# Token units of a fused four-layer network: second row products moved ahead of the scores, and encodings, statistics and loads moved behind the maxima

## The chip, the cores and the metric

The kernel runs on one core of a Trainium2 chip: TensorE (PE) multiplies matrices and writes PSUM, VectorE (DVE) and ScalarE (ACT) copy, subtract and normalize, GpSimd (POOL) does part of the splitting, SyncE (SP) issues the DMAs. The metric is device time in microseconds of the whole kernel, lower is better. Before the change the median of 3 runs is 2311.41 us (2311.12 to 2314.84).

## The reference

Two blocks of a network over 4 sequences of 512 positions; the code holds them as 8 halves of 256 tokens (`B, S = 8, 256`), each with its own causal attention. The change lies in the first part, four layers of attention over one-hot token codes plus position codes:

```python
enc = one_hot(token_ids) + sinusoidal_pe
def layer(enc, ws):
    wq, wk = ws
    q = enc @ wq
    k = enc @ wk
    sims = einsum('bqd,bkd->bqk', q, k) * scale
    sims = where(causal_mask, -1e9, sims)
    attn = softmax(sims, axis=-1)
    return einsum('bqk,bkd->bqd', attn, enc)
# four layers in a row, then
h = h + recurrent_attention(layernorm(h))
h = h + ternary_ffn(layernorm(h))
h = h + block_attention(layernorm(h))
h = h + table_ffn(layernorm(h))
```

## The kernel before

**Precision.** Every matrix product works on float16 pairs, a high half (ScalarE's copy) and a low half (VectorE's or GpSimd's subtraction of the high half from the float32 value), in three passes. So each product waits for a ScalarE copy and a subtraction behind it.

**Token units.** The 2048 tokens are 4 chunks c of 512. The four layers l of a chunk are units, 16 in all, in the order of the table `TOK`: (0,0) (0,1) (1,0) (0,2) (1,1) (2,0) (0,3) (1,2) (3,0) (2,1) (1,3) (2,2) (3,1) (2,3) (3,2) (3,3), as (l, c); unit 9 is (2,1). The layer's result is not formed; instead the attention matrices of a chunk are multiplied up (`tok_pt`), and each layer's q and k come from that product and "row products", encodings times the layer's weights (`tok_ew`, two halves b = 0 and 1, the second into PSUM bank 7). A token output (`tok_out`) multiplies the last product with the encodings of a chunk; `OUT_AT` places the four of them.

**One unit u, as each engine has it written out by hand.** The engines run their own lists in order and meet through semaphores.
- TensorE (`tok_pe`): project q and k of unit u+1 (`tok_project`, L461 and L464, or L250 for layer 0); first row products of u (L491, waits for the probabilities of u where it uses bank 2); transpose the probabilities of u (L272); scores of u+1 (`tok_scores`, L1523 and L1529, wait for `k_split`); second row products (L491); product of attention matrices (`tok_pt`, L507 to L511).
- ScalarE (`tok_act`): copies of q, k; outputs; encoding copies; a sum of |w| (`tok_act_abs`, L1621) in eight units, in units 1 and 6 (`ABS_LATE`) behind the exponential; first rows' copy (L1594); pT copy (L353); the split of a 1 MB weight piece in two halves (`rw_split_act`, L1501); second rows' copy (L1594); the exponential (`act_exp`, L305 and L307); the copy of `tok_pt`'s result (L1616).
- VectorE (`tok_dve`): low halves of q and k (L285, L289); column encodings (`cols_dve`, L1719); first rows' subtraction (L1708); pT's (L357); the mask and maxima of unit u+1 (`dve_max`, L295 to L299); second rows' subtraction; normalizing (`dve_norm`, L312 to L318, or `dve_norm_rows`, L399 to L412, for layer 0); the subtraction that ends `tok_pt` (L1743); column subtractions (`cols_lo`, L1727); row encodings (`rows_dve`, L1735; 2, 3, 3, 4, 4 in units 3 to 7); layer norm statistics (L574 to L582) and, in unit 12, mixing (L1461, L1471) for the next stage.
- GpSimd: low halves of the row encodings and of the weight piece (L1508). SyncE (queue SPq): per unit the next weight piece's two loads (L1883), its store (L1898), the 1 MB load for the sum of |w| (L1889), and the transposing DMAs of the probabilities (`sp_turn`, L386), four of 128x384 a turn.

Behind the units stands the recurrent attention stage, whose products (L749) bring TensorE to 99% busy. Its weights come by `load_rw`, a table lookup's indices by `load_idx`.

## Time and profile before

| | |
|---|---|
| median of 3 runs | 2311.41 us |
| profiled execution | 2310.06 us, span 2308.1 us |
| TensorE | busy 2232.7 us (97%) |
| VectorE | 1647.9 us (71%) |
| ScalarE | 718.5 us (31%) |
| GpSimd | 375.9 us (16%) |
| TensorE clock granted | 0.993 of full speed over the span |

The page divides the span in 40 slices of 57.7 us. TensorE has 6, 8, 7, 7 and 8 tenths in the first five and 9 or more in all others, so the time that can be won on it lies in the first 250 us: the token units. There DMA engines are busy 78% and ScalarE has two thirds of its stage filled.

### The profile page before, as it was taken

To read this page: it belongs to the slowest core of one execution; us is meant where nothing else is said; L and a number is where in the kernel's file an instruction comes from. 1 tells how busy PE (TensorE), PEld (TensorE's weight loads), DVE (VectorE), ACT (ScalarE), POOL (GpSimd) and SP (SyncE) were. 2 spreads that over 40 slices of the span, in tenths; PEclk is the share of its full clock that TensorE was granted. 3 is DMA by queue.
4 is the path that set the end of the run, shared out by engine and by line. 5 is a ranking of instruction groups with operands and counts; after the bars stand their busy time and mean duration, and the time that the engine had idled before them with its cause. 6 is when DMAs were issued, how large, how long until landed. Compare 5 with 4: busy or idle time off the path is not lost.

```text
span 2308.1 us, 31300 instructions
## 1 busy us (share of the span) xinstructions
PE 2232.7 (97%) x12058; PEld 1141.7 (49%) x12058; DVE 1647.9 (71%) x3357; ACT 718.5 (31%) x1603; POOL 375.9 (16%) x416
## 2 busy tenths in 40 slices
PE   6877899999999999999999999999999999999999
PEld 4666444444444444444445555555555555444444
DVE  7667799998998886577766665665665667688832
ACT  5666313122122122444333333233233233211111
POOL 3453100000000330541050002200300300401000
PEclk9999999999999999999999999999999999999999
DMA  6877533323332341120131112311311222100001
GB/s 171 264 194 206 216 132 119 128 96 119 133 120 93 142 154 67 44 85 12 51 94 35 35 30 52 89 31 32 107 33 31 71 46 35 60 1 1 1 1 74
DMA packets 171109, 196.47 MB, mean 85 GB/s; under 512 B 124368, under 2 KB 137296, under 8 KB 162000
## 3 DMA queue, kind: packets, MB, share of 16 engines
q1 hardware_dynamic: 170672, 193.41, 28.0%
q8 instruction: 96, 1.57, 0.3%
q10 hardware_dynamic: 288, 1.05, 0.1%
q14 instruction: 53, 0.43, 0.1%
HBM read 137.28 MB, written 27.26 MB: 71 GB/s over the span
## 4 chain that ended last, share of the span: by engine, by line
PE 85%; DVE 5%; issue 3%; ACT 2%; DMA 2%; POOL 1%; SPq 1%; DVEq 0%; POOLq 0%
PE ps L749 21%; PE ps L250 14%; PE ps L1370 10%; PE ps L761 7%; PE ps L1186 7%; PE ps L1173 7%; PE ps L642 5%; PE ps L1000 4%; PE ps L1017 3%; PE ps L1211 2%; PE ps L264 2%; PE ps L607 1%; PE ps L491 1%; SPq L386 1%; PE ps L1214 1%
## 5 line engine op out<-in xcount | busy, mean ns | idle before, releaser
L749 PE MATMUL ps<-planes 128*128 128x512 f16 x1224 | 270.0, 379 | 0.2 <-DVE work L806 0.2
L749 PE MATMUL ps<-planes,wa 128*128 128x512 f16 x1080 | 237.8, 379 | 0.4 <-DVE planes L1476 0.4
L250 PE MATMUL ps<-planes,wa 128*128 128x512 f16 x840 | 192.3, 379 | 3.2 <-DVE planes L1727 3.2
L749 PEld LDWEIGHTS ps<-planes 128*128 128x128 f16 x1224 | 119.6, 98 | 142.2 <-DVE work L806 1.1
L789 ACT ACTIVATE work<-work 128x512 f16<-128x512 f32 x64 | 40.3, 630 | 440.4 <-DVE work L822 440.4
L250 PE MATMUL ps<-planes 128*128 128x512 f16 x768 | 175.9, 379 | 0.9 <-DVE planes L622 0.9
L749 PEld LDWEIGHTS ps<-planes,wa 128*128 128x128 f16 x1080 | 105.6, 98 | 125.8 <-ACT h L1589 0.9
L305 ACT ACTIVATE ps<-ps,nmax 128x128 f32<-128x128 f32 x160 | 54.5, 341 | 307.0 <-DVE nmax L299 306.9
L587 POOL TENSOR_TENSOR rstd<-rstd,half 128x4 f32<-128x4 f32 x16 | 17.9, 1118 | 770.6 <-DVE rstd L582 770.5
L904 DVE COPY_PREDICATED work<-work 128x1024 f32<-128x1024 int16 x144 | 119.5, 830 | 20.9
L886 DVE TENSOR_SCALAR work<-work,lutx,par 128x256 int32<-128x256 int32 x384 | 128.0, 406 | 0.0
L250 PEld LDWEIGHTS ps<-planes,wa 128*128 128x128 f16 x840 | 80.6, 98 | 87.8 <-DVE planes L1727 3.8
L1017 PE MATMUL ps<-wa,work 128*128 128x512 f16 x512 | 120.9, 379 | 0.0
L1000 PE MATMUL ps<-planes,wa 128*128 128x512 f16 x512 | 120.6, 379 | 0.0
L1370 PE MATMUL ps<-planes 128*128 128x512 f16 x528 | 117.4, 379 | 0.0
L1370 PE MATMUL ps<-planes,wa 128*128 128x512 f16 x528 | 116.6, 379 | 0.0
L250 PEld LDWEIGHTS ps<-planes 128*128 128x128 f16 x768 | 73.8, 98 | 78.3 <-DVE planes L622 1.4
L1292 DVE TENSOR_TENSOR planes<-ps,planes 128x512 f16<-128x512 f32 x64 | 44.2, 691 | 81.0 <-ACT planes L1266 81.0
L970 POOL TENSOR_SCALAR planes<-stg 128x512 f16<-128x512 f32 x44 | 28.2, 669 | 446.3 <-PE ps L1186 368.6
L326 DVE RECIPROCAL rinv<-rsum 128x4 f32<-128x4 f32 x64 | 11.4, 178 | 117.5 <-ACT ps L307 115.4
L1298 DVE TENSOR_TENSOR h<-ps,h 128x512 f32<-128x512 f32 x64 | 44.2, 691 | 71.4 <-PE ps L1186 67.5
L761 PE MATMUL ps<-planes,work 128*128 128x512 f16 x408 | 93.6, 379 | 0.0
(195 smaller groups left out, 4242.4 us busy)
## 6 DMA issues: line engine op xcount, KB each, us to landing
planes<-rw SPq DMA_DIRECT2D x17, 2048.0 KB, 8.3
wa<-rw SPq DMA_DIRECT2D x15, 2048.0 KB, 7.3
stg<-in_rw_w SPq DMA_DIRECT2D x32, 512.0 KB, 5.6
stg<-in_ff_w SPq DMA_DIRECT2D x16, 1024.0 KB, 5.3
rw<-wa SPq DMA_DIRECT2D x16, 1024.0 KB, 8.0
stg<-in_mo_w SPq DMA_DIRECT2D x16, 1024.0 KB, 5.7
work<-in_glu_idx SPq DMA_DIRECT2D x48, 128.0 KB, 2.1
glu_dec<-work SPq DMA_DIRECT2D x48, 128.0 KB, 1.7
```

Source lines behind the costliest of these rows:

```text
L250: mm = te.matmul(ps[:, bank, :], w(i, kt), x(j, kt), start=(kt == 0 and n == 0), stop=(kt == KT - 1 and n == 2))
L305: se.activation(x, x, ACT.Exp, bias=nmax[:, b:b + 1], accum_out=rsum[:, b:b + 1])
L642: mm = te.matmul(ps[:, bank, :], x, y, start=(m == 0), stop=(m == len(pairs) - 1))
L749: mm = te.matmul(ps[:, what, :], rw_w(q, what, i, kt, m), mix[what][j][:, kt, at:at + CH], start=(kt == 0 and z == 0), stop=(kt == KT - 1 ...
L761: mm = te.matmul(ps[:, 4 + j, :], oT[t % 4][x][:, j * P:j * P + P], rw_wo(q, y, m), start=(n == 0 and z == 0), stop=(n == HEADS - 1 and z ...
L886: return ve.tensor_scalar(dec_v[:, j, :].bitcast(I32), dec_idx, lutx[:, j:j + 1], lut[:, 2 * j:2 * j + 1], ALU.bitwise_and, ALU.bitwise_xor)
L904: ins = ve.copy_predicated(pairs[:, :, 0, :], mask, pairs[:, :, 1, :])
L1000: mm = te.matmul(ps[:, t % 3, :], slot[:, at:at + P], tokT[x][:, kt, c * CH:c * CH + CH], start=(kt == 0 and x == 0), stop=(kt == KT - 1 a ...
L1017: mm = te.matmul(ps[:, 4 + j, :], gT[t % FF_BUF][x][:, j * P:j * P + P], slot[:, PW + m * D:PW + m * D + D], start=(k == 0 and x == 0), st ...
L1173: mm = te.matmul(ps[:, bank, :], tokT[x][:, kt, tt * P:tt * P + P], halves(slot, 2)[y][:, kt * CH:kt * CH + CH], start=(kt == 0 and z == 0 ...
L1186: mm = te.matmul(ps[:, FB, :], x, y, start=(z == 0), stop=(z == len(pairs) - 1))
L1370: mm = te.matmul(ps[:, 2 * (n % 2) + piece, :], glu_halves(g, piece)[i][:, at:at + P], tokT[j][:, kt, c * CH:c * CH + CH], start=(kt == 0 ...
```

## The change

1. TensorE: the second row products stand ahead of the scores of unit u+1. VectorE: the second rows' subtraction stands ahead of the maxima.
2. VectorE: column subtractions, row encodings and the layer norm statistics (moved from unit 9 to unit 10) stand between the maxima and the normalizing; the mixing of unit 12 stands behind the normalizing and `tok_pt`'s subtraction, and its two ScalarE copies behind `tok_pt`'s copy.
3. The probabilities' planes have another layout (768 contiguous columns for both sequences of a chunk), so a turn is two transposes of 128x768 instead of four of 128x384.
4. Unit 14's transposes write banks 6 and 7 and no longer wait for the previous `tok_pt`.
5. SyncE: in iterations 1 and 6 the load for the sum of |w| goes behind the weight loads and the store; weight pair 1 of the next stage is loaded after the last token output and the first index load.

```diff
@@ pe_transpose_probs, act_pT, dve_pT @@
+        def pT_bank(u):
+            return 6 if u == LAYERS * NC - 2 else 4
...
-                    mm = te.transpose(ps[:, 4 + b, i * P:i * P + P], prob[:, at:at + P], ident[:, :])
+                    mm = te.transpose(ps[:, pT_bank(u) + b, i * P:i * P + P], prob[:, at:at + P], ident[:, :])
@@ layout and transposes @@
+        def p_turn(half_, c, which):
+
+            at = c * NTOK + CH + which * 768
+            return planes[:, 4 + half_, at:at + 768]
...
             for half_ in range(2):
-                for b in range(2):
-                    dst = act_T(4 + half_)[:, 2 * b + 1 - src, c * CH:c * CH + 384].rearrange("p (n q) -> p n q", n=3)
-                    sp.dma_start_transpose(dst, act_T(4 + half_)[:, 2 * b + src, c * CH:c * CH + 384]).then_inc(done, 16)
+                sp.dma_start_transpose(p_turn(half_, c, 1 - src).rearrange("p (n q) -> p n q", n=6), p_turn(half_, c, src)).then_inc(done, 16)
@@ tok_pe @@
-                tok_scores(pe, u + 1, 2 * nth(l, c, (0, 1, 2)) - 1 if l < LAYERS - 1 and ew_bank(u, 0) == 2 else 0)
                 if l < LAYERS - 1:
                     tok_ew(pe, u, 1)
+                tok_scores(pe, u + 1, 2 * nth(l, c, (0, 1, 2)) - 1 if l < LAYERS - 1 and ew_bank(u, 0) == 2 else 0)
...
             u = MU - 2
+            pe.wait_ge(ew_lo, 2 * nth(*TOK[u - 1], (0, 1, 2)))
+            pe.wait_ge(to_free, 2 * TPC)
+            pe_transpose_probs(pe, u)
             pe.wait_ge(pt_lo, nth(*TOK[u - 1], (1, 2, 3)))
-            pe_transpose_probs(pe, u)
@@ tok_act @@
-                if u == MU - 4:
-                    mix_hi_act(act, 0)
-                    mix_hi_act(act, 1)
                 if u in ABS_LATE:
                     tok_act_abs(act, ABS_AT.index(u))
                 if l > 0:
                     tok_act_pt(act, u)
+                if u == MU - 4:
+                    mix_hi_act(act, 0)
+                    mix_hi_act(act, 1)
@@ tok_dve @@
                 tok_dve_pT(dve, u)
-                dve_max(dve, u + 1)
-                if u == 1:
-                    cols_lo(dve, COLS_AT[1])
                 if l < LAYERS - 1:
                     tok_dve_ew(dve, u, 1)
-                if u == MU - 4:
-                    mix_diff(dve, 0, 0)
-                    mix_y_dve(dve, 0)
-                    mix_y_dve(dve, 1)
+                dve_max(dve, u + 1)
+                if u > 0:
+                    cols_lo(dve, COLS_AT.get(u, ()))
+                for r in ROWS_AT.get(u, ()):
+                    rows_dve(dve, r)
+                if u == OUT_AT[0] + 1:
+                    dve.wait_ge(to_free, TPC)
+                    ln_dve_chunk(dve, 0, 0, chain)
                 tok_dve_norm(dve, u + 1)
                 if l > 0:
                     tok_dve_pt(dve, u)
-                if u > 1:
-                    cols_lo(dve, COLS_AT.get(u, ()))
-                for r in ROWS_AT.get(u, ()):
-                    rows_dve(dve, r)
-                if u == OUT_AT[0]:
-                    dve.wait_ge(to_free, TPC)
-                    ln_dve_chunk(dve, 0, 0, chain)
...
                 if u == MU - 4:
+                    mix_diff(dve, 0, 0)
+                    mix_y_dve(dve, 0)
+                    mix_y_dve(dve, 1)
                     mix_lo_dve(dve, 0)
@@ sync: load_rw and the loop of weight pieces @@
-                        sp.wait_ge(to_ps, 3 * TPC)
+                        sp.wait_ge(to_ps, NT)
...
-                if j in ABS_AT[:-1]:
+                if j in ABS_AT[:-1] and j not in ABS_LATE:
                     sp.wait_ge(abs_done, ABS_AT.index(j) + 1)
                     load_abs(ABS_AT.index(j) + 1)
...
                 store_rw(j)
+                if j in ABS_LATE:
+                    sp.wait_ge(abs_done, ABS_AT.index(j) + 1)
+                    load_abs(ABS_AT.index(j) + 1)
...
-            load_rw(1)
             store_rw(RW_PIECES - 1)
...
-            load_rw(2)
             sp.wait_ge(mix_lo, 12)
             sp.wait_ge(to_free, NT)
             load_idx(0)
+            load_rw(1)
+            load_rw(2)
             load_rw(3)
```

In the changed kernel the lines are shifted: L1708 is L1719, L1727 is L1738, L1735 is L1746, L295 to L299 are L301 to L305, L491 is L500, L1523 is L1532, L1529 is L1538.

VectorE in unit 1, before: low halves of q and k, two column encodings, the first rows' subtraction, then the maxima and two column subtractions, and only then the second rows' subtraction.

```order
L285 SCALAR_TENSOR_TENSOR work<-ps,work 128x512
L289 TENSOR_TENSOR work<-ps,work 128x512
L1719 SCALAR_TENSOR_TENSOR work<-h,work 128x512 x2
L1708 TENSOR_TENSOR h<-ps,h 128x2x256
L295 TENSOR_TENSOR ps<-ps,causal 128x256
L295 TENSOR_TENSOR ps<-ps,causal 128x2x128
L298 TENSOR_REDUCE nmax<-ps 128x2
L299 TENSOR_REDUCE nmax<-ps 128x2
L1727 TENSOR_TENSOR planes<-work,planes 128x512 x2
L1708 TENSOR_TENSOR h<-ps,h 128x2x256
```

After:

```order
L291 SCALAR_TENSOR_TENSOR work<-ps,work 128x512
L295 TENSOR_TENSOR work<-ps,work 128x512
L1730 SCALAR_TENSOR_TENSOR work<-h,work 128x512 x2
L1719 TENSOR_TENSOR h<-ps,h 128x2x256 x2
L301 TENSOR_TENSOR ps<-ps,causal 128x256
L301 TENSOR_TENSOR ps<-ps,causal 128x2x128
L304 TENSOR_REDUCE nmax<-ps 128x2
L305 TENSOR_REDUCE nmax<-ps 128x2
L1738 TENSOR_TENSOR planes<-work,planes 128x512 x2
```

Both subtractions of the row products now stand in one row, ahead of the maxima.

VectorE in unit 7 around the normalizing of unit 8, before: maxima, second rows' subtraction, reciprocal and normalizing, the subtraction of `tok_pt`, and the last four row encodings (L1735) ahead of the low halves of q and k of unit 9.

```order
L295 TENSOR_TENSOR ps<-ps,causal 128x256
L295 TENSOR_TENSOR ps<-ps,causal 128x2x128
L298 TENSOR_REDUCE nmax<-ps 128x2
L299 TENSOR_REDUCE nmax<-ps 128x2
L1708 TENSOR_TENSOR h<-ps,h 128x2x256
L312 RECIPROCAL rinv<-rsum 128x4
L316 TENSOR_TENSOR work<-ps,rinv 128x2x128
L318 TENSOR_TENSOR work<-ps,rinv 128x2x256
L1743 TENSOR_TENSOR planes<-ps,planes 128x2x384
L1735 SCALAR_TENSOR_TENSOR work<-work 128x512 x4
L285 SCALAR_TENSOR_TENSOR work<-ps,work 128x512
L289 TENSOR_TENSOR work<-ps,work 128x512
```

After, the four encodings (L1746) stand between the maxima and the reciprocal:

```order
L1719 TENSOR_TENSOR h<-ps,h 128x2x256
L301 TENSOR_TENSOR ps<-ps,causal 128x256
L301 TENSOR_TENSOR ps<-ps,causal 128x2x128
L304 TENSOR_REDUCE nmax<-ps 128x2
L305 TENSOR_REDUCE nmax<-ps 128x2
L1746 SCALAR_TENSOR_TENSOR work<-work 128x512 x4
L318 RECIPROCAL rinv<-rsum 128x4
L322 TENSOR_TENSOR work<-ps,rinv 128x2x128
L324 TENSOR_TENSOR work<-ps,rinv 128x2x256
L1754 TENSOR_TENSOR planes<-ps,planes 128x768
L291 SCALAR_TENSOR_TENSOR work<-ps,work 128x512
L295 TENSOR_TENSOR work<-ps,work 128x512
```

What moved is four encodings, from between normalizing and q and k to between maxima and normalizing.

TensorE in unit 5 (row products of the unit around the transposes and scores), before:

```order
L250 MATMUL ps<-planes,wa 128x512 x24
L491 MATMUL ps<-wa,planes 128x256 x24
L272 MATMUL ps<-ident,work 128x128 x6
L1523 MATMUL ps<-work 128x256 x6
L1529 MATMUL ps<-work 128x128 x6
L491 MATMUL ps<-wa,planes 128x256 x24
L507 MATMUL ps<-work,planes 128x256 x3
```

After:

```order
L250 MATMUL ps<-planes,wa 128x512 x24
L500 MATMUL ps<-wa,planes 128x256 x24
L278 MATMUL ps<-ident,work 128x128 x6
L500 MATMUL ps<-wa,planes 128x256 x24
L1532 MATMUL ps<-work 128x256 x6
L1538 MATMUL ps<-work 128x128 x6
L516 MATMUL ps<-work,planes 128x256 x3
```

The 24 matmuls of the second row products now stand between the transposes and the scores.

## Rows read from the trace of the kernel before

**Rows 1.** Busy time by stretch: start:end us, its length, then each engine's busy us

```profile
0.00:250.80 250.80, 187.44 (x1530) 141.24 (x1531) 177.43 (x313) 162.11 (x325) 105.98 (x93) 0.93 0.78 218
250.80:2308.10 2057.30, 2045.25 (x10528) 1000.45 (x10528) 1470.44 (x3044) 556.39 (x1279) 269.88 (x324) 1.00 0.23 69
```

**Rows 2.** Who TensorE waited for, first 300 us: us in total, times, longest us

```profile
PE ps L1523 <- DVE work L289: 13.8, 10, 4.0
...
PE ps L539 <- DVE planes L1743: 7.0, 3, 4.9
```

**Rows 3.** Timeline of unit 9: start us, us, engine, line, tiles, count [idle before <- releaser]

```profile
156.49 2.78 PE L491 MATMUL ps<-wa,planes 128*128 128x256 f16 x24
...
159.11 0.82 PE L272 MATMUL ps<-ident,work 128*128 128x128 f32 x6
...
167.58 2.78 PE L491 MATMUL ps<-wa,planes 128*128 128x256 f16 x24 [0.46 <-DVE work L318]
...
160.67 1.99 ACT L1501 ACTIVATE wa<-stg 128x1024 f16<-128x1024 f32 x2
...
163.85 0.60 ACT L1594 ACTIVATE h<-ps 128x512 f16<-128x512 f32 x1 [1.19 <-PE ps L491]
...
165.84 0.22 ACT L307 ACTIVATION_READ_ACCUMULATOR ps<-ps,nmax 128x1 f32 x1
...
161.68 0.76 DVE L295 TENSOR_TENSOR ps<-ps,causal 128x256 f32<-128x256 f32 x2
...
162.81 0.68 DVE L299 TENSOR_REDUCE nmax<-ps 128x2 f32<-128x512 f32 x1
```

**Rows 4.** Transposes (ns min/median/max), a wait for a load, the page's landing time

```profile
L386 SPq DMA_TRANSPOSE planes<-planes x48: 1197/1260/2856, 30.5 to 229.4; - x48
...
L347 SPq DMA_TRANSPOSE work<-work x64: 1274/1432/2318, 1182.3 to 1949.0; - x64
...
89.84 1.91 ACT L1621 ACTIVATE stg<-stg 128x2048 f32<-128x2048 f32 x1 [2.91 <-DMA stg<-in_ff_w]
...
planes<-rw SPq DMA_DIRECT2D x17, 2048.0 KB, 8.3
```

**Rows 5.** Timeline of VectorE: encodings twice, statistics, mixing

```profile
124.25 2.73 DVE L1735 SCALAR_TENSOR_TENSOR work<-work 128x512 f32<-128x512 f32 x4
...
139.67 3.63 DVE L1735 SCALAR_TENSOR_TENSOR work<-work 128x512 f32<-128x512 f32 x4
...
168.11 2.46 DVE L574 BATCH_NORM_STATS2 stat<-h 128x6 f32<-128x512 f32 x4
...
201.62 3.08 DVE L1471 SCALAR_TENSOR_TENSOR work<-work,par 128x512 f32<-128x512 f32 x2
```

**Rows 6.** Timeline of TensorE: landmarks of the token stage

```profile
72.12 2.78 PE L491 MATMUL ps<-wa,planes 128*128 128x256 f16 x24 [2.90 <-DVE planes L412]
...
87.61 1.37 PE L1523 MATMUL ps<-work 128*128 128x256 f16 x6 [2.13 <-DVE work L289]
...
100.59 2.78 PE L491 MATMUL ps<-wa,planes 128*128 128x256 f16 x24
...
144.64 1.44 PE L1523 MATMUL ps<-work 128*128 128x256 f16 x6 [3.96 <-DVE work L289]
...
180.06 2.78 PE L491 MATMUL ps<-wa,planes 128*128 128x256 f16 x24 [0.46 <-DVE work L318]
...
207.20 5.71 PE L539 MATMUL ps<-planes 128*128 128x512 f16 x18 [4.94 <-DVE planes L1743]
...
250.81 15.70 PE L749 MATMUL ps<-planes,wa 128*128 128x512 f16 x72 [0.43 <-DVE planes L1476]
```

**Rows 7.** Timeline of unit 1: ScalarE, VectorE, and TensorE's next project

```profile
50.11 1.06 ACT L1501 ACTIVATE wa<-stg 128x1024 f16<-128x1024 f32 x1 [2.04 <-DMA stg<-in_rw_w]
...
46.73 0.76 DVE L295 TENSOR_TENSOR ps<-ps,causal 128x256 f32<-128x256 f32 x2
...
51.47 5.35 PE L250 MATMUL ps<-planes,wa 128*128 128x512 f16 x24 [2.41 <-DVE planes L1727]
```

More of the change, by code:

```diff
@@ L265, in pe_scores, with pT_view @@
             mm.then_inc(scored, 1)
+        def pT_bank(u):
+            return 6 if u == LAYERS * NC - 2 else 4
+        def pT_view(u):
+            return ps[:, pT_bank(u):pT_bank(u) + 2, 0:384]
         def pe_transpose_probs(pe, u):
@@ L347, in sp_pT @@
             sp.dma_start_transpose(pT_all, prob_all).then_inc(pT_in, 16)
-        pT_view = ps[:, 4:6, 0:384]
+        pt_view = ps[:, 4:6, 0:384]
         def act_pT(act, u):
             act.wait_ge(pT_ps, nth(*TOK[u], (1, 2, 3)))
-            se.activation(pT[0].rearrange("p (b k) -> p b k", b=2), pT_view, ACT.Copy).then_inc(pT_hi, 1)
+            se.activation(pT[0].rearrange("p (b k) -> p b k", b=2), pT_view(u), ACT.Copy).then_inc(pT_hi, 1)
         def dve_pT(dve, u):
             dve.wait_ge(pT_hi, nth(*TOK[u], (1, 2, 3)))
-            ve.tensor_tensor(pT[1].rearrange("p (b k) -> p b k", b=2), pT_view,
+            ve.tensor_tensor(pT[1].rearrange("p (b k) -> p b k", b=2), pT_view(u),
                              pT[0].rearrange("p (b k) -> p b k", b=2), ALU.subtract).then_inc(pT_split, 1)
@@ L376, in build @@
         TOK_W = wa[:, 8192:16384].rearrange("p (i l q k d) -> p i l q k d", i=2, l=LAYERS, q=2, k=KT)
+        def p_turn(half_, c, which):
+            at = c * NTOK + CH + which * 768
+            return planes[:, 4 + half_, at:at + 768]
         def chunk_rows(half_, c, which):
-            return act_T(4 + half_)[:, which:which + 3:2, c * CH:c * CH + 384]
+            return p_turn(half_, c, which).rearrange("p (b k) -> p b k", b=2)
         def sp_turn(sp, c, src, done):
             for half_ in range(2):
-                for b in range(2):
-                    dst = act_T(4 + half_)[:, 2 * b + 1 - src, c * CH:c * CH + 384].rearrange("p (n q) -> p n q", n=3)
-                    sp.dma_start_transpose(dst, act_T(4 + half_)[:, 2 * b + src, c * CH:c * CH + 384]).then_inc(done, 16)
+                sp.dma_start_transpose(p_turn(half_, c, 1 - src).rearrange("p (n q) -> p n q", n=6), p_turn(half_, c, src)).then_inc(done, 16)
         def sp_p1(sp, u):
@@ L422, in p_rows @@
         def p_rows(half_, c, b):
-            return act_T(4 + half_)[:, 2 * b, c * CH:c * CH + 384]
+            return p_turn(half_, c, 0)[:, b * 384:b * 384 + 384]
         def p_cols(half_, c, b):
-            return act_T(4 + half_)[:, 2 * b + 1, c * CH:c * CH + 384]
+            return p_turn(half_, c, 1)[:, b * 384:b * 384 + 384]
         def ew_tile(l, half_, tt):
@@ L453, in tok_project @@
             if l == 1:
-                pe.wait_ge(p1T_in[c], 64)
+                pe.wait_ge(p1T_in[c], 32)
             else:
@@ L502, in tok_pt @@
             else:
-                pe.wait_ge(pr_in[c], 64 * (l - 1))
+                pe.wait_ge(pr_in[c], 32 * (l - 1))
             for b in range(2):
@@ L1615, in tok_act_pt @@
             act.wait_ge(pt_ps, nth(*TOK[u], (1, 2, 3)))
-            se.activation(chunk_rows(0, TOK[u][1], 1), pT_view, ACT.Copy).then_inc(pt_hi, 1)
+            se.activation(chunk_rows(0, TOK[u][1], 1), pt_view, ACT.Copy).then_inc(pt_hi, 1)
         def tok_act_abs(act, k):
@@ L2041, in _ @@
                 rw_split_pool(pool, u)
-                if u == OUT_AT[0]:
+                if u == OUT_AT[0] + 1:
                     ln_pool_chunk(pool, 0, 0)
```

2 lines of the change are left out of this document (1 added, 1 removed).

## The prediction, made before the changed kernel ran

> **What bounds the kernel now.** I read four views. First the busy time by stretch: the change lies in the first 250.8 us, the token stage, where TensorE is busy 187.44 of 250.80 us at a mean granted clock of 0.93; in the 2057.30 us behind it TensorE is busy 99% and nothing is moved there that it waits for [rows 1]. So the question is how much of the 63 us of idle time and of the low clock goes. Second, who waits for whom: TensorE's largest repeated wait is at the scores, which need VectorE's low half of k: 13.8 us in 10 waits [rows 2], and into it the change puts row products, 2.78 us a unit (2.63 from start to the next start) [rows 3]. Third, the timeline of one unit that has no such wait (unit 9, [rows 3]): what closes its loop. Fourth, TensorE's landmarks over the stage [rows 6], which my sum runs along.
>
> In unit 9 before, from the start of the first row products (156.49) to the same point of unit 10 (167.58) it takes 11.1 us. ScalarE takes the rows' copy, pT and the two halves of the weight split (160.67, 1.99 us), and then stands until TensorE has ended the second row products (163.85); only behind that copy does the exponential begin. VectorE's maxima (161.68 to 162.81 + 0.60 = 163.4) were done beside it, hidden. The exponential ends at 166.06, and behind VectorE's normalizing TensorE goes on at 167.58 [rows 3].
>
> **The change part by part.** *Row products before the scores, their subtraction before the maxima.* No instruction more or less. In the new order unit 9 goes: first rows' end 2.63 us after their start (159.12), ScalarE's copy, pT and split end as now at 162.66; the second rows are then done (156.49 + 2.63 + 0.66 + 2.63 = 162.4, the transposes at 0.82 less what overlaps), so the copy runs 162.66 to 163.26; VectorE's subtraction 0.69 (as its maxima's second instruction of the same size, 0.68), 163.95; scores are ready (162.4 + 1.2 = 163.6); maxima 1.74 (161.68 to 163.42 before), 165.7; exponential 1.7 (from the copy's end at 164.4 to 166.06), 167.4; normalizing and the signal to TensorE 1.5 (166.06 to 167.58), 168.9 [rows 3]. Overlaps of neighbouring instructions take some 0.1 off: the loop is 12.4 us instead of 11.1. So every unit with row products pays 1.3 us, since the maxima, once hidden, now stand on the loop behind ScalarE's split; it earns back its own wait at the scores, up to 2.63 us.
>
> *Work behind the maxima.* Encodings, column subtractions and the statistics now lie under the exponential, which covers 1.74 us. Four encodings take 3.63 us beside GpSimd, 0.91 each, while four others took 2.73, 0.68 each [rows 5]; I take 0.68 to 0.9. Statistics take 2.46 and some 0.5 for two short steps, 3.0 us [rows 5]. What exceeds 1.74 spills: 0.9 in unit 3 (two subtractions, two encodings, 2.6), 0.3 in units 4 and 5, 1.0 in unit 6, 1.5 in unit 7, 1.2 in unit 10. But they no longer stand ahead of the next q and k.
> On the 3.63 the Trainium skill (SBUF — State Buffer, "Who interferes with whom") says that a VectorE instruction with two SBUF inputs contends with a GpSimd instruction that reads SBUF. By it all moved encodings that meet GpSimd's split would run at the long time, some 1 us more a unit in units 5 to 7, which is the slow rival below.
>
> *Transposes.* 24 issues instead of 48. Issue time: 1260 ns for 384 columns, 1432 ns for 1536 [rows 4]; at 768 I take 1.3, with 2.5 (in proportion) as the upper end and 1.26 as the lower. SP then gives 2.6 us instead of 5.2 a turn. The first turn holds TensorE now and would land some 2 us earlier, but the next thing that holds TensorE (unit 1, below) does not hang on it, so on the path it is worth 0 us. With 2.5 each SP is as late as now: 0 to +1.5 us.
> The Trainium skill (DMA: Bandwidth & Descriptors) tells in its table on transposes between SBUF tensors that earlier generations push one command per tile, 32 cycles a tile. Twelve tiles against three cost 172 ns more here, so the trace agrees in kind; by it a six-tile issue would be some 1.34 us, and the sum stays.
>
> *Loads.* The weight loads go before the load for the sums of |w| in iterations 1 and 6. ScalarE waits for that load twice, in units 2 and 4, the second time 2.91 us [rows 4]: the first stays (its load follows a sum that now comes later), the second goes, as SP is free in time. The load of the second weight pair waits for the last token tile and goes behind the first index load; the product that reads it starts behind 72 others, at 250.81 + 15.70 = 266.5 [rows 6], and issued at about 253 with a landing of 8.3 us [rows 4] it has 5 us to spare: 0 us. The index load goes earlier by about 3 us; TensorE is busy there without a gap, so 0 us.
>
> **The sum along TensorE's landmarks** [rows 6]; each is the time before plus the running difference.
> *Unit 1: +3.9.* Here the reorder costs most. VectorE had maxima at 46.73 and the column subtractions right behind, which TensorE's project at 51.47 waits for. Now the second rows' subtraction stands ahead of both, and its copy on ScalarE waits behind a weight half that lands at 50.1: 51.65 [rows 7]. Then 0.69 + 1.74 + 1.3 (two column subtractions of the same size, GpSimd done by then): 55.4 with the signal instead of 51.47. TensorE then stands some 9 us and will run at the lower clock for a while; that lies in the wait of unit 2, so I count 0, upper end +2.
> *Unit 2: +1.3*, no wait to earn. *Unit 3: +0.8*: 1.3 + 0.9 spill − 1.4 of waits. Running +6.0.
> *Unit 4: −4.4.* TensorE's own chain bound it: a wait of 2.13 before the scores, low clock behind it (six take 1.37, as against 0.8 elsewhere; 1.8 with the row products behind them), 1.0 for the pT delayed by the load [rows 4, 6]; against a new wait of 0.5 at the end. Running +1.6.
> *Units 5 and 6: +1.6 and +0.3.* Running +3.5.
> *Units 7 and 8: −3.5.* The four encodings of 3.63 us stood before q and k of unit 9, so that its scores waited until 144.64 [rows 5, 6]; this goes, less the spill and 1.3. Running 0.
> *Unit 9: +1.0. Unit 10: +1.2* (statistics spill; its scores' wait of 1.5 is paid out in the loop). Running +2.2 at 180.06. *Unit 11: −1.1*: there the exponential waits for the layer norm transposes anyway, so the maxima are hidden.
> *Unit 12: −2.9.* The mixing (to 201.62 + 3.08 = 204.7 [rows 5]) stood before the normalizing; now behind. The token output starts at 205.4, not 207.20. Running −1.8.
> *Unit 13: +3.1.* The mixing is now ahead of the copies, ScalarE's outputs wait for it as before (each output sits behind a mixing copy), a 1.9 us sum of |w| follows, and then the new order costs its 1.3. It gives nearly all back; running +1.3 at the normalizing of unit 14. *Unit 14: −1.0*: its transposes no longer wait for the previous subtraction. Running +0.3, and this reaches 250.81.
>
> 3.9 + 1.3 + 0.8 − 4.4 + 1.6 + 0.3 − 3.5 + 1.0 + 1.2 − 1.1 − 2.9 + 3.1 − 1.0 = +0.3. The profiled execution took 2310.06 us, 1.96 beside its span; with +0.3 it is 2310.4. The median of the runs is 1.35 above the profiled one, so the forecast is 2311.7 us: no change. About 0.2%, 4.6 us, is what a measurement of this kernel can tell from none.
>
> **The rivals.** *All waits are filled and the maxima stay hidden.* If ScalarE's part of the loop shortens too (its split often waited for weights, and loads now come earlier), the units do not pay 1.3. The nine units from 2 on that have second rows, but for unit 11, times 1.3 is 11.7 us off, and unit 1 may be 2 less: 2298; half of it 2304. For it: 13.8 us of waits, 7.0 more at the token output [rows 2]. Against: in unit 9 the split did not wait and the loop still closes through it. Chance 0.29.
> *Spill: the work behind the maxima delays the normalizing (slower).* In units 3 to 7 and 10 the moved work runs beside GpSimd's split, each instruction at 0.91 or more instead of 0.68; with 17 such instructions and 4 subtractions, 21 × 0.25 = 5, and 2 of low clock in unit 1: 2319. It decides as soon as VectorE reaches the reciprocal more than 1.74 us after its maxima. For it: 3.63 for four, 2.46 for the statistics [rows 5]. Against: GpSimd's split ends before the late part. Chance 0.22.
> *The change does not do what it says* in units 0 (already so), 8, 12, 14 and 15, which have no second row products: true, and in the sum.
> The forecast's case has 0.49.
>
> **How the numbers follow.** The forecast's case spans 2306 to 2317 (each unit ±0.4 over thirteen, and the two ends of transposes and clock). The range reaches into both rivals: 2301 to 2320. Faster by over 0.2% needs under 2306.8: the first rival and an edge of the forecast, 0.31. Slower needs over 2316: 0.22. Within: 0.47.
>
> **What would show it.** Right: the scores' waits of 13.8 us fall below 4; waits on the normalizing's output (before the first rows or the transposes) rise to over 12; the project of unit 2's iteration starts near 55, token output 1 near 205; transposes issue in about 1.3. In a plain unit the exponential starts about 2.5 us after ScalarE's second row copy has ended. Wrong: if that project starts before 52, unit 1 is mis-sized; if the loop of unit 9 stays at 11.1 us, the first rival holds; if the normalizing in units 5 to 7 starts over 1 us after the exponential's end, the second.

## The result, and the profile after

The kernel after takes 2320.6 us (median of 8 runs, 2317.6 to 2322.4), the kernel before 2311.4 (8 runs, 2310.0 to 2314.8): a ratio of 1.0038, 95% interval 1.0028 to 1.0047. It is slower by 9.2 us. The forecast was 2311.7 with a range of 2301 to 2320, so the result lies just outside it. The two profiled executions, from which all rows come, took 2321.28 and 2310.06 us and so lie 11.2 apart.

First the busy time by stretch of the kernel after, columns as in [rows 1]:

```profile
0.00:262.08 262.08, 191.78 (x1531) 143.76 (x1531) 176.76 (x313) 160.56 (x326) 104.01 (x93) 0.90 0.69 201
262.08:2319.30 2057.22, 2045.26 (x10528) 1000.57 (x10528) 1471.86 (x3044) 555.99 (x1277) 269.28 (x324) 1.00 0.23 70
```

All of it lies in the token stage, which ends at 262.08 in place of 250.81 [rows 1]. The 2057 us behind it have not moved. Of the 11.3 us TensorE is busy 4.3 longer with the same matmuls, at a mean granted clock of 0.90 in place of 0.93, and stands idle 6.9 longer.

Who TensorE waited for after (us in total, times, longest us), first 300 us:

```profile
PE ps L278 <- DVE work L324: 11.8, 4, 5.5
...
PE ps L500 <- DVE planes L421: 9.2, 2, 5.0
PE ps L250 <- DVE planes L1738: 8.0, 2, 7.2
PE ps L278 <- DVE planes L1754: 7.3, 2, 6.2
PE ps L500 <- DVE work L324: 5.5, 3, 3.2
...
PE ps L1532 <- DVE work L295: 2.1, 3, 1.5
```

The same waits before:

```profile
PE ps L491 <- DVE planes L412: 4.8, 2, 2.9
...
PE ps L250 <- DVE planes L1727: 3.2, 2, 2.4
...
PE ps L272 <- DVE work L318: 1.9, 1, 1.9
...
PE ps L491 <- DVE work L318: 0.9, 2, 0.5
```

The wait at the scores went from 13.8 us to 2.1 [rows 2], as foretold. In its place stand longer ones: 26.5 us in place of 7.6 for the normalizing (L324 and L421; into the transposes L278 and the first row products L500), and 8.0 in place of 3.2 for the column subtractions (L1738) at the project (L250), of which 7.2 in unit 1.

TensorE's landmarks after. 79.36, 106.86, 151.42, 190.74, 215.19 and 262.08 are the points that [rows 6] have at 72.12, 100.59, 144.64, 180.06, 207.20 and 250.81; 56.22 is the project of [rows 7], and 164.79 the start of unit 9's row products in [rows 3]:

```profile
56.22 7.58 PE L250 MATMUL ps<-planes,wa 128*128 128x512 f16 x24 [7.21 <-DVE planes L1738]
...
79.36 7.97 PE L500 MATMUL ps<-wa,planes 128*128 128x256 f16 x48 [5.01 <-DVE planes L421]
...
95.61 0.85 PE L278 MATMUL ps<-ident,work 128*128 128x128 f32 x6 [2.69 <-DVE work L324]
...
106.86 2.78 PE L500 MATMUL ps<-wa,planes 128*128 128x256 f16 x24 [0.29 <-DVE work L324]
...
121.37 7.07 PE L500 MATMUL ps<-wa,planes 128*128 128x256 f16 x48 [4.16 <-DVE planes L421]
...
150.08 1.54 PE L278 MATMUL ps<-ident,work 128*128 128x128 f32 x6 [6.16 <-DVE planes L1754]
...
151.42 1.49 PE L1532 MATMUL ps<-work 128*128 128x256 f16 x6
...
159.22 5.73 PE L548 MATMUL ps<-planes 128*128 128x512 f16 x18 [2.23 <-DVE planes L1754]
164.79 2.78 PE L500 MATMUL ps<-wa,planes 128*128 128x256 f16 x24
...
177.21 2.78 PE L500 MATMUL ps<-wa,planes 128*128 128x256 f16 x24 [2.07 <-DVE work L324]
...
190.74 4.29 PE L500 MATMUL ps<-wa,planes 128*128 128x256 f16 x24 [3.18 <-DVE work L324]
...
215.19 3.40 PE L548 MATMUL ps<-planes 128*128 128x512 f16 x15 [2.23 <-DVE planes L1754]
...
262.08 15.70 PE L758 MATMUL ps<-planes,wa 128*128 128x512 f16 x72 [0.74 <-ACT h L1600]
```

Two more rows of the kernel before, the transposes of unit 4 and the token output of unit 9:

```profile
84.67 0.82 PE L272 MATMUL ps<-ident,work 128*128 128x128 f32 x6
...
152.60 4.04 PE L539 MATMUL ps<-planes 128*128 128x512 f16 x18 [1.34 <-DVE planes L1743]
```

Read the second column (how long the group took) beside the wait in the brackets. The project takes 7.58 us behind a wait of 7.21, where [rows 7] have 5.35 behind 2.41. 48 row products take 7.97 and 7.07 us behind waits of 5.01 and 4.16; where the clock is up, 48 take 5.40 (e4 below). Six transposes take 1.54, not 0.87, and the token output 5.73, not 4.04. In those two stretches of row products, and around the project, the granted clock by window was 0.67, 0.76 and 0.71: a part of each group ran at 1.2 GHz and the rest at 2.4.

And unit 1, whose entry in the sum, +3.9, was the largest on the side of loss: ScalarE's second row copy, VectorE's subtraction behind it, and the column subtractions that the project waits for:

```profile
51.93 0.58 ACT L1605 ACTIVATE h<-ps 128x512 f16<-128x512 f32 x1
...
52.54 0.69 DVE L1719 TENSOR_TENSOR h<-ps,h 128x512 f16<-128x512 f32 x1 [5.79 <-ACT h L1605]
...
54.88 1.28 DVE L1738 TENSOR_TENSOR planes<-work,planes 128x512 f16<-128x512 f32 x2
```

### The profile page after: what moved, and what is told of

Same layout as the page of the kernel before. It is cut to its first block, busy times and chain, and to the rows that moved or that the text cites. A ratio compares the mean times of both kernels' runs of the same rounds, so it can differ in the third digit from the quotient of the medians.

```text
span 2319.3 us, 31281 instructions
## 1 busy us (share of the span) xinstructions
PE 2237.0 (96%) x12058; PEld 1144.3 (49%) x12058; DVE 1648.6 (71%) x3357; ACT 716.5 (31%) x1603; POOL 373.3 (16%) x416
## 4 chain that ended last, share of the span: by engine, by line
PE 86%; DVE 5%; ACT 4%; issue 3%; DMA 1%; POOL 1%; SPq 0%; DVEq 0%; POOLq 0%; ACTq 0%
PE ps L758 21%; PE ps L250 14%; PE ps L1379 10%; PE ps L770 7%; PE ps L1195 7%; PE ps L1182 7%; PE ps L651 5%; PE ps L1009 4%; PE ps L1026 3%; PE ps L1220 2%; PE ps L264 2%; PE ps L500 1%; PE ps L616 1%; PE ps L1223 1%; PE ps L262 1%
## 5 line engine op out<-in xcount | busy, mean ns | idle before, releaser
L250 PE MATMUL ps<-planes,wa 128*128 128x512 f16 x840 | 194.5, 382 | 8.0 <-DVE planes L1738 8.0
L250 PE MATMUL ps<-planes 128*128 128x512 f16 x768 | 175.9, 379 | 0.9 <-DVE planes L631 0.9
L250 PEld LDWEIGHTS ps<-planes,wa 128*128 128x128 f16 x840 | 81.2, 99 | 94.1 <-DVE planes L1738 8.5
L250 PEld LDWEIGHTS ps<-planes 128*128 128x128 f16 x768 | 73.8, 98 | 78.3 <-DVE planes L631 1.4
```

The lines of the kernel that those rows point to most:

```text
L250: mm = te.matmul(ps[:, bank, :], w(i, kt), x(j, kt), start=(kt == 0 and n == 0), stop=(kt == KT - 1 and n == 2))
```

## The experiments

Sixteen kernels, each against runs of the kernel before on the same chip. "Before" was 2310.6 to 2311.7 us in all of them. A "filler" is a matmul whose result nobody reads. The table below has, for the kernels before and after and five of the sixteen, the time in us from the start of ScalarE's exponential of unit u to that of unit u+1, read from the timeline of ScalarE. The last step goes from exponential 15 to the first product behind the stage.

| step of unit | before | after | e6 | e4 | e1 | e3 | e15 |
|---|---|---|---|---|---|---|---|
| 1 | 14.93 | 18.19 | 15.49 | 17.59 | 15.27 | 15.62 | 15.47 |
| 2 | 15.89 | 19.70 | 19.03 | 18.67 | 19.81 | 19.20 | 15.43 |
| 3 | 13.32 | 16.48 | 13.83 | 13.98 | 13.41 | 13.32 | 13.32 |
| 4 | 15.02 | 11.75 | 13.35 | 12.68 | 11.46 | 12.82 | 11.99 |
| 5 | 12.67 | 13.11 | 13.39 | 13.39 | 13.68 | 13.67 | 13.78 |
| 6 | 12.91 | 15.52 | 15.52 | 13.85 | 16.18 | 12.90 | 12.90 |
| 7 | 14.55 | 12.71 | 10.84 | 12.70 | 10.58 | 11.27 | 12.93 |
| 8 | 12.70 | 10.97 | 13.73 | 10.30 | 13.77 | 12.70 | 12.71 |
| 9 | 15.74 | 18.74 | 16.82 | 17.05 | 17.41 | 15.74 | 15.73 |
| 10 | 12.47 | 12.42 | 12.17 | 12.41 | 11.09 | 12.48 | 12.48 |
| 11 | 15.30 | 16.42 | 19.26 | 16.55 | 17.27 | 15.29 | 15.29 |
| 13 | 20.11 | 20.12 | 18.51 | 20.12 | 18.99 | 21.09 | 19.00 |
| 14 | 13.31 | 12.83 | 12.65 | 12.89 | 12.63 | 13.44 | 12.64 |
| end | 16.90 | 17.94 | 17.92 | 17.94 | 16.97 | 16.69 | 17.02 |

(Unit 0 takes 12.98 and unit 12 8.37 in all.) Each column is one execution, and a step can differ by chance. In e7, below, every engine has the instructions of the kernel before up to unit 12, and yet its unit 5 took 14.32 us where before has 12.67. So a difference of 1.7 in one step proves little; the medians of the runs carry the verdicts.

**e1: the order back, the moves kept.** The kernel after with

```diff
-                if l < LAYERS - 1: tok_ew(pe, u, 1)
                 tok_scores(pe, u + 1, ...)
+                if l < LAYERS - 1: tok_ew(pe, u, 1)
...
-                if l < LAYERS - 1: tok_dve_ew(dve, u, 1)
                 dve_max(dve, u + 1)
+                if u == 1: cols_lo(dve, COLS_AT[1])
+                if l < LAYERS - 1: tok_dve_ew(dve, u, 1)
```

> The kernel after, with the old order of the two parts that the change swapped: TensorE takes the next unit's scores before the second row products, and VectorE the maxima before the second rows' subtraction (in unit 1 the encodings' subtractions stand right behind the maxima, as before). The moved encodings, statistics, mixing, loads and the two-transpose form stay. Theory A (the order and the TensorE clock that its longer waits cost are the loss; the moved work fits behind the maxima): the loss of 9.2 us goes and a little more, 2304 to 2312 us. Rival B (the moved encodings behind the maxima hold up the normalizing and are the loss): it stays slow, 2316 to 2321 us. Rival C (transposes or loads): the same 2316 to 2321.

Measured: 2313.4 us, ratio 1.0009 (1.0000 to 1.0018). That lies outside both expectations, 1.4 us over the first. Seven of the 9 us are the order. The spill as the whole cause falls; but the kernel isn't below before, so something among the moves costs as well.

**e2: the order back in unit 1 alone.** The same edit under `if u == 1`.

> The kernel after, with the old order in unit 1 alone, on TensorE and VectorE. The ledger had unit 1 at +3.9 us, without the lower clock of the project behind it (7.58 us in place of 5.35). Theory A: 4 to 6 us less than after, 2314.5 to 2316.5 us, with the project of unit 3 back near 51.5 and at 5.4 us. Rival B (spill in later units absorbs it): under 2 us less than after, 2319 to 2321 us.

Measured: 2317.3 us, 1.0023 (1.0012 to 1.0034), 3.3 less than after, between the two. In its trace the project started at 50.50 and took 5.35, 5.7 us earlier; but unit 2 then took 21.09 in place of 19.70, and the row products of unit 3 took 8.27. (That profiled execution, 2321.2 us, was the slowest of seven, 3.9 over their median.) What ate most of the gain in unit 2 is a load, by this trace: ScalarE stood for the feed-forward piece that the change had moved behind the row weights' loads:

```profile
63.25 1.91 ACT L1635 ACTIVATE stg<-stg 128x2048 f32<-128x2048 f32 x1 [6.77 <-DMA stg<-in_ff_w]
```

In the kernel after the same piece is waited for 1.17 us, since TensorE is late there itself; e9 and e10 take the load up.

**e4: the waits filled with matmuls.**

```diff
+            for z in range(FILL[u]):      # {3: 40, 6: 34, 8: 48}
+                te.matmul(ps[:, 6, 0:S]..., tokT[0][:, 0, 0:P], TOK_W[:, 0, 3, :, 0, :], start=True, stop=True)
...
+                if u == 1:
+                    for z in range(30):
+                        te.matmul(ps[:, 0, :], TOK_W[:, 0, 0, 0, 0, :], tokT[0][:, 0, 0:CH], start=True, stop=True)
```

> The kernel after, with matmuls whose result nobody reads put on TensorE into four of its waits: 30 of 512 columns ahead of the project of unit 3 (a wait of 7.2 us), 40, 34 of 256 columns ahead of the first row products of units 3 and 6 (5.0 and 4.2 us) and 48 ahead of the transposes of unit 8 (6.2 us). At the full clock they take about 6.4, 4.3, 3.7 and 5.2 us, less than the waits. Theory A (the clock that the longer waits cost is the part of the loss that the ledger counted as nothing): the project, row products and transposes behind them run at the full clock, 7.58 -> 5.35, 7.97 -> 5.4, 7.07 -> 5.4, and of these 5 to 6 us most reach the end: 2314 to 2317 us. Rival D (the work behind the waits is slow for another reason, or its length is hidden by VectorE and ScalarE): within 1.5 us of after, 2319 to 2322 us. Cost of a filler that runs past its wait: up to 2 us slower.

Measured: 2314.0 us, 1.0010 (1.0002 to 1.0019). Its timeline of TensorE, fillers (L1550) and landmarks:

```profile
55.61 5.35 PE L250 MATMUL ps<-planes,wa 128*128 128x512 f16 x24
...
72.56 4.53 PE L1550 MATMUL ps<-wa,planes 128*128 128x256 f16 x40
77.72 5.40 PE L500 MATMUL ps<-wa,planes 128*128 128x256 f16 x48 [0.64 <-DVE planes L421]
...
114.11 3.87 PE L1550 MATMUL ps<-wa,planes 128*128 128x256 f16 x34
118.43 5.40 PE L500 MATMUL ps<-wa,planes 128*128 128x256 f16 x48 [0.44 <-DVE planes L421]
...
139.15 5.40 PE L1550 MATMUL ps<-wa,planes 128*128 128x256 f16 x48
...
153.94 4.04 PE L548 MATMUL ps<-planes 128*128 128x512 f16 x18 [2.22 <-DVE planes L1769]
...
183.77 4.42 PE L500 MATMUL ps<-wa,planes 128*128 128x256 f16 x24 [3.18 <-DVE work L324]
...
255.28 15.70 PE L758 MATMUL ps<-planes,wa 128*128 128x512 f16 x72 [0.71 <-ACT h L1615]
```

These extra 152 matmuls do nothing but keep TensorE at work, and the stage ends 6.8 us earlier. TensorE is busy 203.91 us in it; less the fillers' 20.4 by their rows, its own work takes some 183.5 us (an estimate) where after has 191.78. The steps tell where the end gains: units 1 and 2 (-1.6), 3 (-2.5), 4 (+0.9), 6 (-1.7), 8 and 9 (-2.4). Where nothing was filled (unit 11) the group behind a wait of 3.18 us is still slow, 4.42. So TensorE's clock behind the waits is a cause; filling four of them is worth 6.6 us.

Not all of a slow group's time reaches the end. The project at 55.61 takes 2.2 us less than after's at 56.22, but unit 2's step is only 1.0 shorter, because ScalarE now stands longer for the feed-forward piece (2.37 us, after 1.17):

```profile
63.97 1.91 ACT L1647 ACTIVATE stg<-stg 128x2048 f32<-128x2048 f32 x1 [2.37 <-DMA stg<-in_ff_w]
```

Nor can a slow group be put down to one wait. The token output of unit 9 takes 4.04 here and 5.73 in after, behind the same wait of 2.2 us. It is tempting to credit the fill of unit 8's wait, but other runs speak against it. In e12 that wait is filled too, the transposes behind it are fast, and the token output is slow (first fence); in e9 nothing is filled and it is fast behind 2.22 us (second); and in e16 24 row products are slow behind the 2.07 us behind which after has 2.78 (third):

```profile
145.36 0.87 PE L278 MATMUL ps<-ident,work 128*128 128x128 f32 x6 [1.13 <-DVE planes L1772]
...
153.83 5.73 PE L548 MATMUL ps<-planes 128*128 128x512 f16 x18 [2.23 <-DVE planes L1772]
```

```profile
151.19 4.05 PE L548 MATMUL ps<-planes 128*128 128x512 f16 x18 [2.22 <-DVE planes L1752]
```

```profile
173.50 4.45 PE L500 MATMUL ps<-wa,planes 128*128 128x256 f16 x24 [2.07 <-DVE work L324]
```

So the sum of the fills is shown, by medians; the share of unit 9 in it isn't.

**e5: the order alone, on the kernel before.** e1's edit in the other direction.

> The kernel before, with the swap of order alone, on TensorE (second row products, then scores) and on VectorE (second rows' subtraction, then the maxima); encodings, statistics, mixing, loads and transposes stay where they were. Theory A (the order is the loss): 2319 to 2326 us, at or above the kernel after, since nothing is moved behind the maxima to pay for it. Rival B (the moved encodings are the loss, not the order): 2309 to 2313 us.

Measured: 2326.3 us, 1.0064 (1.0051 to 1.0077): 14.6 us over before. That is 0.3 us past the upper end of the first expectation. The order alone costs more than the whole change; the rest of the change pays about 6 us back.

**e3: transposes and loads alone.** The kernel after with TensorE's, ScalarE's and VectorE's order of before.

> The kernel before in its own order on TensorE, VectorE and ScalarE, with the two wide transposes in place of four and the moved loads alone. The old-order kernel with every move of the change stood at 2313.4 us, 1.7 over the kernel before; either these parts cost it or the work moved behind the maxima. Theory A (the moved work behind the maxima costs those 1.7 us, the transposes and loads nothing, as forecast): 2310.5 to 2312.5 us. Rival C (transposes or loads cost it): 2313 to 2315 us.

Measured: 2308.4 us, 0.9989 (0.9980 to 0.9997): a gain of 2.6 us, outside both expectations. So these parts help, and in the old order the moved work costs the difference to e1, 5 us by the medians: units 6 (16.18 to 12.90), 9 and 11. In units 4, 10, 13 and 14 the moved work is ahead by 0.8 to 2.1 each; the two profiled executions are only 2.3 us apart.

**e6: VectorE's old order alone.**

> The kernel after, with VectorE alone in the old order (the maxima before the second rows' subtraction, in unit 1 the encodings right behind the maxima); TensorE keeps the new one. The sum made the loop 1.3 us longer per unit because the maxima stand behind ScalarE's copy and VectorE's subtraction of the second rows. Theory A, if that is so: the scores end 1.3 us after the second row products, the copy and the subtraction some 2.5 us after them, so the loop of a unit of four row-product blocks gets about 1 us shorter (12.4 -> 11.4) and the stage 4 to 7 us shorter: 2314 to 2317 us. Rival E (the later scores on TensorE set it, VectorE's order does not): 2318 to 2321 us.

Measured: 2316.2 us, 1.0020 (1.0011 to 1.0029), 4.4 less than after; the size came as expected, its place did not. The plain loop (unit 10) went from 12.42 to 12.17 only, so what lengthens it is TensorE's order: e1 differs from e6 in that alone, has 11.09 there, and is 2.8 us shorter in all. (The 12.47 of before in that step have the layer norm statistics in them, which stand ahead of the next q and k there.) The gain is in unit 1 (18.19 to 15.49) and behind it in unit 3, whose row products found the clock up after a shorter wait:

```profile
50.48 5.35 PE L250 MATMUL ps<-planes,wa 128*128 128x512 f16 x24 [3.23 <-DVE planes L1738]
...
76.02 5.40 PE L500 MATMUL ps<-wa,planes 128*128 128x256 f16 x48 [1.94 <-DVE planes L421]
```

**e7 and e8: fillers in the old order.** They stand ahead of two table products of the kernel before, and ahead of six groups of e1. (A table product is what the prediction calls a token output, L539 before and L548 after.)

> The kernel before, with matmuls whose result nobody reads in two of its own waits: 18 of 512 columns ahead of the second chunk's table product (a wait of 4.9 us, the product then takes 5.71 us where the first takes 4.04) and 9 ahead of the last chunk's (a wait of 2.1 us, then 5.73 us). Theory A (the clock after a wait costs 1.7 us at each, and each ends on the path): both products at 4.04 us, 2308 to 2310 us. Rival D (hidden by ScalarE and VectorE, or the waits too short to lower the clock): 2311 to 2313 us.

> The old-order kernel with every move of the change (2313.4 us), with matmuls whose result nobody reads ahead of the second probabilities' product of unit 2 (54 of 256 columns), the first row products of unit 6 (30), the transposes of unit 8 (46), the first two chunks' table products (9 of 512 each) and the last chunk's (9 of 512). At the lower clock these took 4.44, 1.54, 5.73, 5.73 and 5.73 us in that kernel, at the full clock 2.78, 0.87 and 4.04. Theory A: 1.7 + 0.7 + 3 x 1.7 = 7.5 us, most of it on the path: 2306 to 2309 us, faster than the kernel before. Rival D: 2312 to 2314 us.

Measured: e7 2311.3 us, 0.9996 (0.9987 to 1.0005); e8 2313.3, 1.0005 (0.9996 to 1.0014), as e1. The clock did rise, and nothing came of it in the medians. In e7:

```profile
208.53 4.04 PE L539 MATMUL ps<-planes 128*128 128x512 f16 x18 [1.05 <-DVE planes L1758]
...
244.41 4.04 PE L539 MATMUL ps<-planes 128*128 128x512 f16 x18
250.57 17.39 PE L749 MATMUL ps<-planes,wa 128*128 128x512 f16 x72 [2.12 <-DVE planes L1476]
```

Both table products take 4.04 us now, not 5.71 and 5.73. Steps 13, 14 and the end are 1.6 us shorter together than before. Then comes VectorE's mixing (L1476), for which TensorE then stands 2.12 us, and the 72 products behind take 17.39 us in place of 15.70 [rows 6]. In e8 units 6 and 9 gained 1.7 each as expected, and unit 3 lost 2.5 (15.90 for 13.41): its row products ran at the lower clock behind a wait of 3.77 us that was 2.13 in e1. I read from this that a low clock costs only where the slow group is what the next step waits for.

**e9 and e10: the two feed-forward loads back.** The change had put the loads for the sums of |w| in iterations 1 and 6 (the feed-forward pieces) behind the row weights' two loads and the store. In e3's timeline of ScalarE, and in e9's, where they are back:

```profile
63.82 1.91 ACT L1630 ACTIVATE stg<-stg 128x2048 f32<-128x2048 f32 x1 [7.65 <-DMA stg<-in_ff_w]
```

```profile
60.32 1.91 ACT L1630 ACTIVATE stg<-stg 128x2048 f32<-128x2048 f32 x1 [2.96 <-DMA stg<-in_ff_w]
...
131.89 2.22 ACT L1510 ACTIVATE wa<-stg 128x1024 f16<-128x1024 f32 x2 [4.04 <-DMA stg<-in_rw_w]
```

> The kernel with the two wide transposes and moved loads alone (2308.4 us), with the two feed-forward pieces that the change had put behind a row-weight piece and its store back at their old places. In its trace ScalarE stood 7.65 us in unit 2 for the feed-forward piece, which landed at 63.8 us where it landed at 60.4 before, and unit 2 took 19.20 us in place of 15.89. Theory F (the later feed-forward load is a loss of its own of up to 3.3 us, inside the change too): 2305 to 2307.5 us. Rival G (the load would land as late, the transposes or the queue hold it, or what is gained is given back): 2308 to 2310 us.

> The kernel after, with the two feed-forward pieces back at their old places alone. There the wait for the piece in unit 2 was only 1.17 us, because TensorE was late itself. Theory F: 0.5 to 1.5 us less than after, 2319 to 2320 us, hard to tell from nothing. Rival H (the row-weight pieces, now later, are what ScalarE waits for in turn): 2321 us or more.

Measured: e9 2309.4 us, 0.9986 (0.9977 to 0.9995), the same as e3 within the intervals; e10 2322.1, 1.0041 (1.0028 to 1.0054). So e9's gain of up to 3.3 us did not come. The first moved load costs 3.6 us in unit 2 (19.20 to 15.58), the second gains 3.2 in unit 7 (11.27 for 14.49), because ScalarE's weight split there no longer stands 4.04 us for its piece. In e10 unit 2 fell to 18.79 and unit 3 to 15.38, while unit 7 rose from 12.71 to 17.08 with a wait of 4.06.

**e11, e15: a kernel from the parts that pay.** Old order; wide transposes; encodings behind the maxima in unit 4 alone; the mixing and the second-last unit's transposes as in the change. e11 has both feed-forward loads at their old places, e15 only the second one moved; the later weight pairs stay moved in both:

```diff
-                if j in ABS_AT[:-1] and j not in ABS_LATE:
+                if j in ABS_AT[:-1] and j != 6:
```

> A candidate: the old order on TensorE and VectorE, the wide transposes, the feed-forward loads at their old places, the encodings moved behind the maxima in unit 4 alone (there the old-order kernel with the moves was 1.36 us shorter), the mixing moved and the second-last unit's transposes ahead (units 13 and 14 were 2.9 us shorter). Theory A: 2308.4 - 3.3 - 1.4 - 2.9, of which some is given back, 2301 to 2306 us. Rival: the gains are not additive, since the same DMA queue and VectorE's mixing catch up: 2307 to 2310 us.

> The candidate (2307.2 us) with the feed-forward piece of unit 6 alone moved behind the row weights, as the change has it, that of unit 1 at its old place. In the candidate's trace unit 7 took 14.40 us with a wait of ScalarE for row weights, which with the moved load was 11.27. Theory F (the two moved loads work against each other, the later one gains 3.2 us): 2303 to 2305.5 us. Rival G (given back later): 2306.5 to 2308.5 us.

Measured: e11 2307.2 us, 0.9983 (0.9974 to 0.9992), so the gains do not simply add up; e15 2304.5, 0.9973 (0.9963 to 0.9982): 6.1 us below the kernel before and 16 below the kernel after. In e15's profile the token stage ends at 245.16:

```profile
0.00:245.16 245.16, 184.93 (x1530) 140.13 (x1531) 176.11 (x313) 160.98 (x325) 106.36 (x93) 0.94 0.73 215
```

TensorE is busy 184.93 us, 6.9 less than after, for the same matmuls.

**e12: three causes out together, TensorE's order kept.** VectorE's old order, fillers in units 1, 6, 8 and 11, old loads.

> The kernel after, with TensorE's new order kept, but the three causes found so far taken out together: VectorE in the old order (alone worth 4.4 us), matmuls whose result nobody reads in TensorE's waits (12 of 512 columns in unit 1, 30 of 256 in unit 6, 50 in unit 8, 26 in unit 11), and the feed-forward loads at their old places. Theory A+F (clock, VectorE's order and the load make up the whole loss, while some of the clock's part is already gone with VectorE's order): 2308 to 2312 us. Rival I (the causes are one and the same, so that removing the second gives nothing): 2314 to 2317 us, as with VectorE's order alone.

Measured: 2313.5 us, 1.0012 (1.0003 to 1.0021), between the two expectations. Alone, VectorE's order was worth 4.4 and the fills 6.6; together they are worth 7.1. So they overlap: in unit 3 the row products take 5.40 behind 2.13 us with no filler. The third part did not help: with the old loads ScalarE stands 4.09 us for row weights in unit 7, which takes 14.53 in place of 12.71. How much of the missing 4 us is overlap and how much this load, no run separates.

**e13, e14: the encodings back, the new order kept.** In units 6 and 7, and in units 2 to 7, they stand behind the probabilities' product again.

> The kernel after, with the encodings of units 6 and 7 back behind the probabilities' product, where they were before. Rival B, the spill (those of four pieces took 3.07 and 3.60 us where the exponential covers 2.5, and held the normalizing up): 2317 to 2319.5 us. Theory A (in the new order nothing else fits behind the maxima, so the place is paid for elsewhere): 2320.5 to 2324 us, slower than after, since order alone, without any of the moves, was 2326.3.

> The same with the encodings of units 2 to 7 back. Theory A: 2321 to 2326 us; rival B: 2315 to 2319 us.

Measured: e13 2320.3 us, 1.0041 (1.0028 to 1.0053); e14 2322.1, 1.0046 (1.0033 to 1.0058). Neither is faster than after; e13 lies between its expectations. In e13 unit 8 took 12.71 in place of 10.97: what the normalizing gains, the next q and k lose. The spill is real. After has, on VectorE in unit 7,

```profile
144.14 3.88 DVE L1746 SCALAR_TENSOR_TENSOR work<-work 128x512 f32<-128x512 f32 x4
147.94 0.16 DVE L318 RECIPROCAL rinv<-rsum 128x4 f32<-128x4 f32 x1
```

with the reciprocal 2.0 us behind the exponential's end (144.26 + 1.7), the sign that the prediction gave for this rival; but taking the spill away gains nothing.

**e16: the kernel after with the second load alone moved.**

> The kernel after, with the feed-forward piece of unit 1 at its old place and that of unit 6 where the change put it. With both back, units 2 and 3 took 18.79 and 15.38 us in place of 19.70 and 16.48, and unit 7 17.08 in place of 12.71. Theory F: 2.0 us less than after, 2317.5 to 2319.5 us. Rival G: 2320 to 2322 us.

Measured: 2319.6 us, 1.0037 (1.0025 to 1.0050): 1.0 less than after, which can't be told from nothing. Its step of unit 2 was 19.24, not 18.79 as in e10.

## Why the prediction was wrong

Most of what the forecast described did happen: the waits moved where it said, and the plain loop grew by what it said. What failed is the price of TensorE's clock. The sum books 1.8 us of it as a gain in unit 4 and 0 for unit 1, and has no term at all for the groups behind the longer waits that it foretold. By its own steps, along the landmarks of the profiled executions:

- *The step that failed:* "TensorE then stands some 9 us and will run at the lower clock for a while; that lies in the wait of unit 2, so I count 0, upper end +2", and nothing for the clock in units 3, 6, 9 and 11. In the rows, the groups there take longer than at the full clock: 2.6 us (48 row products of unit 3), 1.7 (48 of unit 6), 1.7 (token output of unit 9) and 1.5 (24 row products of unit 11, over the 2.78 of [rows 6]). In e4, filling four waits gave 6.6 us back and led to 2314.0, inside the forecast case's own 2306 to 2317. For unit 1 by itself the step was half right: the project took 2.2 us longer, and by e4 1.0 of it reached the end of unit 2, within the upper end. The waits behind the normalizing are where the sum went wrong.
- *Scores' waits under 4, normalizing waits over 12:* 2.1 and 26.5. Right in kind; that the second became twice the bound is the first sign of the miss.
- *Plain loop 12.4 us in place of 11.1:* right, 164.79 to 177.21 is 12.42. The reason given was in part wrong: e6 shows that VectorE's order is only 0.25 of the 1.3. The scores' later end on TensorE is the rest.
- *Unit 1, +3.9, and unit 2, +1.3:* the column subtractions were foretold to let the project go at 55.4 and did at 56.22, a difference of +4.75 to before. At the next landmark (79.36 for 72.12) it was +7.24, foretold +5.2; 0.85 of the 2.0 over had come before the project.
- *Units 3 and 4, +0.8 and −4.4:* −1.0 in sum (+7.24 to +6.27), foretold −3.6; 2.6 is the clock of unit 3. Unit 4's own part came as foretold: its transposes stood at 95.61 for 84.67 before, the next landmark at 106.86 for 100.59, which is −4.7. *Units 5 to 8, −1.6:* +0.5 (scores at 151.42 for 144.64); unit 6 alone 1.7 of clock. *Units 9 and 10, +2.2:* +3.9, 1.7 of clock in this execution. *Units 11 and 12, −4.0:* −2.7 (token output at 215.19 for 207.20), 1.5 of clock. *Units 13 and 14, +2.1:* +3.3; where the other 1.2 is I did not settle.
- *Transposes 0, loads 0:* the issue times were right (median 1326 ns). The zeros were not: together they gain 2.6 us in the old order (e3); there the first load lost 3.6 and the second gained 3.2, so that with both back as before (e9) 1.8 us of gain remain, from the transposes and the later loads of weight pairs, which no run separates. The forecast looked for ScalarE's waits for the feed-forward pieces and missed the one for row weights in unit 7. In the new order most of this is hidden by TensorE's own lateness (e10, e16), so it is not the miss.
- *Work behind the maxima:* as the rival of 0.22 had it, the time went to 2319 or over, yet by another road. The rival's spill exists but isn't worth anything net (e13, e14); its 2 us of low clock was the part that grew.
- *The first rival*, hidden maxima, is out by the loop of 12.42.
- Two figures of the prediction are a little off, and nothing hangs on them: the last maxima instruction of [rows 3] took 0.68 us, not 0.60, and half of the first rival's gain gives 2304.9, not 2304.

What stays open: how the 9.2 us split exactly. Out one at a time, order is worth 7.2, VectorE's part of it 4.4, the four fills 6.6; they overlap (e12). The price of the clock in a single unit is open too, since the same wait left the same group at either clock in different runs. That the order costs 14.6 us without the moves and 7.2 with them says that the parts can't be priced apart from one another.

## What to carry to other kernels

Look at the lengths of the waits that a reorder leaves, and give the clock behind the long ones a term of its own. Here 13.8 us in ten waits gave way to fewer waits of 4 to 7 us; TensorE was busy 4.3 us longer with the same matmuls, and filling four of the waits gave 6.6 us back. The maxima were free only as long as they ran beside ScalarE's weight split; with row products put ahead of the scores, they start later and stand on the loop. A load needs the same look: the piece moved in iteration 1 cost 1 us at most while TensorE was late, and ate part of the gain as soon as it was not (e16, e2, e3). And test bundled edits one by one: here the bundle lost 9.2 us while a subset of it gains 6.1.

## What the runs showed of the hardware that was not expected

- Matmuls whose result nobody reads, put into a wait, shorten the groups behind it: 48 row products from 7.97 to 5.40 us (e4), a table product from 5.71 to 4.04 (e7).
- The length of a wait alone does not tell the clock behind it. A table product behind 2.2 us took 5.73 us in after and e12 and 4.04 in e4 and e9; 24 row products behind 2.07 us took 2.78 in after and 4.45 in e16; 48 behind 3.62 us took 5.40 in e5, behind 3.63 us 8.04 in e14.
- Fillers are no general cure: in e7 and e8 the groups got faster by up to 1.7 us each and the kernel did not; in e8 a later group, behind a wait of 3.77 us, ran slower (5.28 us for 24, against 2.78).
- A load issued behind two row-weight loads and a store lands 3.5 us later (63.8 for 60.3), though SyncE issued it at about the same time, 55.5 and 55.4 (e3, e9). The same move in another iteration takes away a wait of 4.04 us on the same engine.
